# Local attention in a software pipeline: exponential, mix, scaling and projection moved to later steps

## The reference, cut to what matters

```
h = shift_token(x)                      # second half of the features from the row before
q, k, v = split(h @ wqkv, 3)            # 8 heads of 64
q, k = rotary_xpos(l2norm(q) * qs, l2norm(k) * ksc)
sim = 8 * q @ k.T                       # within windows of 64 rows
attn = softmax(where(mask, -max, sim))
o = attn @ v                            # per head
x = x + o @ wo
```

## Time and profile before

| | us |
|---|---|
| median of 3 runs | 4570.37 |
| lowest and highest run | 4561.98, 4570.56 |
| the profiled execution's own time | 4563.37 |
| its span in the trace | 4561.6 |
| TensorE busy | 3651.8 (80%) |
| VectorE busy | 2882.0 (63%) |
| ScalarE busy | 1862.3 (41%) |
| GpSimd busy | 1395.2 (31%) |

### The profile page before, as it was taken

How to read it: one execution, slowest core, us unless ns; L and a number is a source line. 1 busy time by engine, 2 the same in 40 slices (tenths; PEclk the granted TensorE clock), 3 DMA queues, 4 the chain that set the end, 5 groups by cost and what they waited for, 6 DMA issues and landing times. The chain is left out here.

```text
span 4561.6 us, 95626 instructions
## 1 busy us (share of the span) xinstructions
PE 3651.8 (80%) x31569; PEld 2350.1 (52%) x31569; DVE 2882.0 (63%) x6293; ACT 1862.3 (41%) x3725; POOL 1395.2 (31%) x1775
## 2 busy tenths in 40 slices
PE   5676299999788497016995999787999898999897
PEld 5444145454566332015664665554666554666654
DVE  3798811111477769887886676566777544777654
ACT  1233222222477416434552222554666423666521
POOL 0676300000133005432441000005767303767500
PEclk9999599999899698558995999558999999999998
DMA  3111000000000000000110000200000000000000
GB/s 95 38 41 33 26 0 0 0 0 0 13 14 13 6 0 0 0 0 26 45 41 15 1 0 0 93 0 23 9 9 9 6 0 20 9 9 9 9 0 37
DMA packets 121910, 73.93 MB, mean 16 GB/s; under 512 B 57172, under 2 KB 117592, under 8 KB 120792
## 3 DMA queue, kind: packets, MB, share of 16 engines
q1 hardware_dynamic: 120376, 72.41, 5.7%
q10 hardware_dynamic: 1440, 0.34, 0.0%
HBM read 60.18 MB, written 4.19 MB: 14 GB/s over the span
## 5 line engine op out<-in xcount | busy, mean ns | idle before, releaser
L2179 POOL TENSOR_TENSOR la_turned<-la_turned,la_sines 128x1024 f32<-128x1024 f32 x128 | 301.9, 2359 | 694.5 <-DVE la_sines L2105 694.5
L790 DVE TENSOR_TENSOR l0f_y<-A,l0f_s 128x512 f32<-128x512 f32 x16 | 11.1, 692 | 463.4 <-PE A L757 463.4
L2173 POOL TENSOR_TENSOR la_scaled<-la_turned,la_rlen 128x1024 f32<-128x1024 f32 x128 | 243.7, 1904 | 17.1 <-POOL la_rlen L2166 13.7
L1948 PE MATMUL A<-l1f_wT,l1f_down_oq 128*128 128x128 f32 x384 | 54.5, 309 | 225.4 <-DVE l1f_down_oq L1909 225.4
L1057 POOL COPY l1x_vd<-half 128x16 f32<-128x16 f32 x8 | 1.2, 213 | 651.0 <-POOLq L47 651.0
L2403 ACT ACTIVATE gg_gate<-B,gg_b 128x512 f32<-128x512 f32 (+1 forms) x96 | 65.8, 686 | 280.8 <-PE B L2434 280.8
L2075 ACT ACTIVATE la_sq<-A 128x1024 f32<-128x1024 f32 x128 | 131.2, 1025 | 106.8 <-PE A L2225 81.9
L2097 DVE TENSOR_TENSOR la_turned<-A,la_cos 128x1024 f32<-128x1024 f32 x128 | 155.7, 1216 | 29.1 <-issue 15.0
L1948 PEld LDWEIGHTS A<-l1f_wT,l1f_down_oq 128*128 128x128 f32 x384 | 51.9, 220 | 229.0 <-DVE l1f_down_oq L1909 214.8
L2059 ACT ACTIVATE la_prob<-la_prob 128x512 f32<-128x512 f32 x128 | 80.7, 630 | 204.1 <-DVE la_prob L2118 204.1
L2115 DVE TENSOR_REDUCE la_top<-B 128x8 f32<-128x512 f32 x128 | 88.6, 692 | 108.2 <-PE B L2238 108.2
(11 more groups left out here) (447 smaller groups left out, 10680.0 us busy)
## 6 DMA issues: line engine op xcount, KB each, us to landing
memory_ctx<-in_ctx SPq DMA_DIRECT2D x128, 64.0 KB, 2.2
l2x_ctx<-in_ctx SPq DMA_DIRECT2D x128, 64.0 KB, 2.2
X<-in_x SPq DMA_DIRECT2D x4, 1024.0 KB, 8.0
gates_ctxT<-in_ctxT SPq DMA_DIRECT2D x16, 256.0 KB, 2.8
memory_ctxT<-in_ctxT SPq DMA_DIRECT2D x64, 64.0 KB, 1.8
l1x_ctxT<-in_ctxT SPq DMA_DIRECT2D x64, 64.0 KB
l2x_ctxT<-in_ctxT SPq DMA_DIRECT2D x64, 64.0 KB
l3x_ctxT<-in_ctxT SPq DMA_DIRECT2D x8, 512.0 KB, 4.2
```

The lines of the kernel that those rows point to most:

```text
L1948: last = pe.matmul(banks[j][0][:, t * P:t * P + P], oq[j][:, o, t * P:t * P + P], wT[:, 2 * F + o], start=(o == 0), stop=(o == F - 1))
L2173: pool.tensor_tensor(by_head(scaled), by_head(turned), spread_heads(rlen[j % 2][:], W3), ALU.mult)\
L2179: pool.tensor_tensor(turned[j % 2][:], turned[j % 2][:], sines[j % 2][:], ALU.add)\
```

## The change

The change gives pieces of the pipeline other lags and another order. `exps` goes one step later (lag 0 to -1), `copy_p`, `turn_p` and `mix` go from -1 to -2, `outputs` from -1 to -3, `turn_o`, `copy_o` and `project` from -2 to -3, and `add` from -2 to -4. `root` keeps its place in the round: it was the last of a step for tile s+2 and is now the first for s+1. On TensorE `make_v` now stands ahead of `turn_o`, and `project` behind `mix`. The projection gets other columns of its bank, which the mixed output does not use, and there are new waits for what is now unfinished: in `turn_p` and `scores` for `shifted`, in `project` for `added`, in `mix` for `o_copied`, in `outputs` for `out_done`.

```diff
--- before.py
+++ after.py
@@ -2001,7 +2001,7 @@
         sim = banks(tried)[:, :, 0:G * S].rearrange("p u (g k) -> p u g k", g=G)
         turned_p = banks(tried)[:, :, G * S:CH]
         out = banks(used)[:, :, 0:G * (W3 + 1)].rearrange("p u (g w) -> p u g w", g=G)
-        turned_o, projected = used[:, 0:CH], used[:, CH:CH + P]
+        turned_o, projected = used[:, 0:CH], used[:, 2 * CH - P:2 * CH]
         turned_h, made_v = keyed[:, CH:CH + P], keyed[:, 0:CH]
         heads = lambda x: x.rearrange("p n (h w) -> p n h w", h=HEADS3)
         made_heads = made[:].rearrange("p (n h w) -> p n h w", n=2, h=HEADS3)
@@ -2078,14 +2078,14 @@
                 act.wait_ge(ones_set, 8)
 
                 def step(it, j):
+                    at4(it, j, 1, root)
                     at4(it, j, 0, copy_qk)
-                    at4(it, j, -1, copy_p)
-                    at4(it, j, -2, copy_o)
+                    at4(it, j, -2, copy_p)
+                    at4(it, j, -1, exps)
+                    at4(it, j, -3, copy_o)
                     at4(it, j, 4, copy_h)
                     at4(it, j, 1, values)
-                    at4(it, j, 0, exps)
                     at4(it, j, 3, squares)
-                    at4(it, j, 2, root)
 
                 steps4(act, step)
 
@@ -2126,6 +2126,7 @@
 
                 def outputs(it, j):
                     dve.wait_ge(mixed, done(it, j))
+                    dve.wait_ge(out_done, done(it, j, 1))
                     dve.reciprocal(inv[j % 2][:], out[:, :, :, W3]).then_inc(inverted, 1)
                     dve.wait_ge(inverted, done(it, j))
                     dve.wait_ge(o_turned, done(it, j, 2))
@@ -2143,11 +2144,11 @@
 
                 def step(it, j):
                     at4(it, j, 2, cosines)
+                    at4(it, j, -3, outputs)
                     at4(it, j, 2, sine_terms)
                     at4(it, j, 0, shift)
-                    at4(it, j, -2, add)
+                    at4(it, j, -4, add)
                     at4(it, j, 2, lengths)
-                    at4(it, j, -1, outputs)
 
                 steps4(dve, step)
 
@@ -2207,6 +2208,7 @@
 
                 def turn_p(it, j):
                     pe.wait_ge(exped, done(it, j))
+                    pe.wait_ge(shifted, ahead(it, j, 1))
                     for g in range(G):
                         last = pe.transpose(turned_p[:, g // 2, g % 2 * P:g % 2 * P + P],
                                             prob[j % 2][:, g].rearrange("p u k -> p (u k)"), m.ident[:])
@@ -2225,7 +2227,8 @@
                     pe.matmul(made[:, CH:2 * CH], hT[j][:], wk[:], start=True, stop=True).then_inc(qk_made, 1)
 
                 def scores(it, j):
-                    pe.wait_ge(p_copied, done(it, j, 1))
+                    pe.wait_ge(p_copied, done(it, j, 2))
+                    pe.wait_ge(shifted, done(it, j, 1))
                     pe.matmul(banks(tried)[:, 0, 0:G * S], m.ident_bf[:], repeat_heads(m.causal_bf[:], G),
                               start=True, stop=False)
                     pe.wait_ge(qk_copied, done(it, j))
@@ -2241,6 +2244,7 @@
 
                 def project(it, j):
                     pe.wait_ge(o_copied, done(it, j))
+                    pe.wait_ge(added, done(it, j, 1))
                     for g in range(G):
                         last = pe.matmul(projected, oT[j % 2][:, g], wo[:, g], start=(g == 0), stop=(g == G - 1))
                     last.then_inc(out_done, 1)
@@ -2263,7 +2267,8 @@
 
                 def mix(it, j):
                     pe.wait_ge(v_kept, done(it, j))
-                    pe.wait_ge(added, done(it, j, 1))
+                    pe.wait_ge(added, done(it, j, 2))
+                    pe.wait_ge(o_copied, done(it, j, 1))
                     pe.wait_ge(p_copied, done(it, j))
                     pe.sem_inc(tiles_free, 1)
                     for g in range(G):
@@ -2279,14 +2284,14 @@
 
                 def step(it, j):
                     at4(it, j, 0, turn_qk)
-                    at4(it, j, -1, turn_p)
-                    at4(it, j, -2, turn_o)
+                    at4(it, j, -2, turn_p)
                     at4(it, j, 1, make_v)
+                    at4(it, j, -3, turn_o)
                     at4(it, j, 4, turn_h)
                     at4(it, j, 0, scores)
-                    at4(it, j, -2, project)
                     at4(it, j, 3, make_qk)
-                    at4(it, j, -1, mix)
+                    at4(it, j, -2, mix)
+                    at4(it, j, -3, project)
 
                 steps4(pe, step)
```

## The result

The changed kernel is slower. Its median is 4630.86 us (4 runs, 4622.71 to 4633.26) against 4567.51 (4 runs, 4561.98 to 4570.56): a ratio of 1.0139, 95% interval 1.0126 to 1.0152. The forecast was 4615, in a range of 4596 to 4634. Its profiled execution took 4631.74 us, 68.4 more than that of before.

A forecast was written before the change was run, and what follows sets the result against it. TensorE's instruction list was taken as the bound. Per layer 21.5 for 58 full steps, -1.6 first steps, +8.3 last steps, -3.3 turns: 24.9 us; two layers, 49.8, on 4563.4 gave 4613.2, said as 4615, range 4596 to 4634.

The forecast's parts named there:

- The bound: Middle of a layer: TensorE's instruction list plays without pause, 7.44 us a step, and the other engines wait for it.
- `make_v`: On TensorE, now ahead of `turn_o`, it waits for ScalarE's copy of q: 0.31 us of stall in each step.
- The list: TensorE's new step laid out: 7.81 us against 7.44, 0.31 of it stall and 0.06 less well placed tile changes.
- `mix` and `add`, with 0.08 to spare: TensorE's `mix` starts 2.55 us behind the scores, VectorE's `add` allows it at 2.47: no cost, 0.08 to spare.
- Rival 2: `mix` waits as well: if VectorE is 0.2 us later, 14 us more, 4629; chance 0.12.
- The turn of the loop: TensorE's 0.25 us at each of 13 turns per layer goes, as the loop turns behind `project`: -3.3 us a layer.
- rival 1: The turn of the loop keeps its cost on TensorE: 2 x 3.3 us more, 4620; chance 0.14.
- First steps: Start of a layer: the first two steps lose pieces to later ones, together -1.6 us.
- Last steps: End of a layer: `project` behind the waiting `mix`, the stall, and one round more for the last tile: +8.3 us.
- The sum: All terms together: 24.9 us per layer, 49.8 for two layers, giving 4613.2, said as 4615.

The follow-up runs named there:

- e9: e6 with `turn_o` moved between the q and k halves of `make_qk` on TensorE; 4540.3 us.
- e1: The changed kernel with ScalarE's copy of q waiting for q's four transposes alone, not also k's; 4589.1 us.
- e3: The kernel before with `make_v` put ahead of `turn_o` on TensorE and nothing else changed; 4606.3 us.
- e5: The changed kernel with the copy of q waiting for q's transposes alone and VectorE's `add` directly behind `outputs`; 4569.6 us.
- e7: e5 with `project` back between the scores and `make_qk`, so that `mix` is last in the step; 4601.7 us.
- e8: The changed kernel with the exponential back at its old lag and place on ScalarE; 4627.3 us.
- e6: e5 with TensorE's 64-wide scores and `mix` side by side, and VectorE's and ScalarE's pieces moved with them; 4555.1 us.

## Why the prediction was right

**The bound.** TensorE's list set the step before the change, as read from the earlier trace rows. e9 shows it from the other side: with two changes of tile less a step is 7.23 us and a layer 12 us shorter than in the kernel before, though VectorE's and ScalarE's pieces stand in other places there too.

**`make_v`.** Right in mechanism, place and size. The forecast was 0.31 a step at a start of 1.72; the earlier trace rows give 1.89 before and the trace after 1.71, with a wait for ScalarE in each step. Taking the wait away gave 42 us back, 37 of them in the full steps, where 37 were expected (e1), and putting it alone into the kernel before cost 39 where 38 were expected (e3).

**The list.** A step of 7.81 was laid out, 7.82 measured; e5, without waits, has 7.49, 0.05 above the 7.44 of the earlier trace rows, which is the 0.06 of tile changes.

**`mix` and `add`, with 0.08 to spare.** Right for ordinary steps. Rival 2 came true at the turns only: there VectorE is 0.19 late in layer 0, more than the 0.08, and `mix` starts 0.17 late; in layer 1 it is 0.09 and 0.07.

**The turn of the loop.** This step failed. I credited 3.3 us a layer, since TensorE's own turn would be hidden behind `project`. TensorE's part was right: no idle time for issue is left, and e7 brings it back by putting `mix` last. But other engines also do something once in a round, and I had asked it of TensorE alone. In place of the gain, ScalarE's copy of q comes 0.07 later after a turn, and VectorE's `add` holds `mix`: four steps of the changed kernel are 7.97 + 7.83 + 7.80 + 7.87 = 31.47 us in layer 0, 0.23 over four times 7.81, and 31.35 in layer 1, 0.11 over; before it was 0.25 in both. Over the 57 full steps of a layer the loss was 21.1 and 19.1 us, where 17.8 had been forecast. That is 4.6 of the 6.6 us of rival 1, and not by its way, since the wait at `make_v` did not bring TensorE's own idle time back.

**First steps.** Forecast -1.6 a layer; up to the fourth tile's scores it was -0.7 in layer 0 and +0.6 in layer 1. In the last 20 us of this part of layer 1 the clock was lower, 0.92 for 1.00, as these busy times show, changed kernel and kernel before:

```profile
3884.00:3904.80 20.80, 18.52 (x210) 11.39 (x209) 15.45 (x20) 11.99 (x27) 16.26 (x22) 0.92 0.05 11
```

```profile
3847.30:3867.70 20.40, 19.41 (x259) 12.77 (x257) 16.54 (x23) 13.68 (x30) 16.39 (x22) 1.00 0.05 12
```

Over the whole part it was 0.86 for 0.87, in layer 0 0.85 for 0.80. How much of the difference is the clock's was not separated, so the -1.6 is not shown.

**Last steps.** The order was right, and the size at the full clock; a term for the clock was missing. From the scores of tile 60 to the last `add` it was 31.4 and 31.2 us before, 41.9 and 42.9 after: +10.5 and +11.7, forecast +8.3. The order of the waits was as laid out: in layer 0's end three waits of 1.8 us of `mix` for `add`, one round more for the last tile:

```profile
PE B L2278 <- DVE l3f_y L2125: 5.3, 3, 1.8
```

At a clock of 1.00 the three steps take 22.4 us (layer 0) and the part behind them 16.6 (e1's layer 0, e8's layer 1), 39.0 together: +7.6 to +7.8. The other 2.9 and 3.9 us are what I had not counted. In the longer and emptier end, with groups of about 1 us and waits of up to 1.8 between them, the clock was at its lower level, 1.2 GHz, from 3624.5 to 3631.4 in layer 0, and from 4361.8 to 4365.2 and from 4372.0 to 4375.5 in layer 1.

**The sum.** 49.8 had been forecast for both layers and 62.3 came: some 5 from the turns in the full steps, 3 from the first steps, 6 from the last ones. With 6 us of other stages this gives 4631. The range held it, since rivals 1 and 2 were in it, but partly by luck: neither the clock nor a difference of 6 us in other stages was among its terms, and 4631 lies near its upper end.

Left open: in the step of e6 shown the copy of the output ended at 3407.42 and `mix` began 0.24 later, where TensorE follows such a copy after 0.05 at `make_v`. Moving the copy closed the gap, so the copy holds `mix`; why this handover is longer is not known. Whether `mix` needs to wait for `added` at all, with the projection in other columns, was not tried, since without that wait `mix` could write to a bank that `add` still reads.

## What to carry to other kernels

In a pipeline that is bound by one engine's list, ask of each moved piece three things: which answer it needs, how long that answer takes from the instruction that asks for it (here 0.27 + 0.04 + 0.59 + 0.05), and how many instructions of the bound engine still stand between. If they are fewer than the answer takes, the difference is paid in every step. Here the cure was to ask sooner, by a semaphore behind the part that is really needed. And what an engine does once in a round of the loop must be looked for on every engine that the bound one waits for.

## What the runs showed of the hardware

In these lists a change from 128-wide to 64-wide products costs TensorE 0.09 us (the next product starts 0.20 after the last one, for 0.11) and the change back 0.10 to 0.11; scores to `mix` side by side take 0.52 from start to start (e9), and scores to anything else 0.62. Once or twice in a round of the loop the other engines are slower to follow. VectorE's subtraction starts 0.81 behind the maximum it needs in two steps of four, 0.72 in the others, and 0.91 in the first step of a round in layer 0 of the changed kernel. ScalarE's copy starts 0.11 after TensorE's last transpose in the first step of a round of the changed kernel and 0.04 in the others (in the kernel before, 0.11 in two steps of four), and the stall follows it: 0.31 and 0.24. And an end of a stage with gaps of up to 1.8 us between short groups can be granted the lower clock or not: 0.77 in the changed kernel, 1.00 in e1 with the same order. What decides between the two, these runs do not show.
